# A two-layer gated mixture-of-experts kernel: the second layer's shared expert as one expert of 704, with its weights as the loaded operand

## The reference

```python
# layer 1, xf is 2048 x 512
y = _moe(xf, gate_w, w1, w2, w3)     # 32 experts of 352 inner columns, top 6 of them per row
shared = jax.nn.silu(xf @ sw1) * (xf @ sw3) @ sw2     # sw1, sw3: 512 x 704, sw2: 704 x 512
return (y + shared).reshape(shape)
```

## Time and profile before

| | |
|---|---|
| Median of 3 runs | 1539.49 us (1535.4 to 1543.76) |
| The profiled execution, own time | 1538.83 us |
| Its span in the trace | 1537.0 us |
| TensorE / weight loads / VectorE / ScalarE / GpSimd busy | 85 / 57 / 71 / 51 / 40 % of the span |
| Mean granted TensorE clock | 0.95 of full speed |
| Matmuls | 9124 |

### The profile page before, as it was taken

How to read it: one execution, slowest core, us unless ns; L and a number is a source line. 1 busy time by engine, 2 the same in 40 slices (tenths; PEclk the granted TensorE clock), 3 DMA queues, 4 the chain that set the end, 5 groups by cost and what they waited for, 6 DMA issues and landing times.

```text
span 1537.0 us, 26168 instructions
## 1 busy us (share of the span) xinstructions
PE 1307.7 (85%) x9124; PEld 880.5 (57%) x9124; DVE 1085.1 (71%) x2186; ACT 780.0 (51%) x1451; POOL 616.2 (40%) x478
## 2 busy tenths in 40 slices
PE   0045665589999599999899999999999999999997
PEld 0023352244444365566577777777777777777775
DVE  8999988988989568888655565556656665666432
ACT  3466664645555544442155555555555555555433
POOL 2243443453442244330134444444444445444432
PEclk9988766999999799999999999999999999999999
DMA  3556645679996676551449999998999999999754
GB/s 105 173 164 198 152 117 129 138 181 183 227 241 171 179 212 194 157 167 44 143 125 193 221 202 206 216 208 210 194 216 209 224 188 218 194 231 191 137 101 53
DMA packets 224191, 269.28 MB, mean 175 GB/s; under 512 B 148608, under 2 KB 148736, under 8 KB 223936
## 3 DMA queue, kind: packets, MB, share of 16 engines
q1 hardware_dynamic: 187408, 175.58, 46.2%
q0 software_dynamic: 36656, 92.03, 29.6%
HBM read 167.87 MB, written 70.32 MB: 155 GB/s over the span
## 4 chain that ended last, share of the span: by engine, by line
PE 70%; DVE 22%; issue 5%; ACT 2%; DMA 1%; POOL 0%; POOLq 0%; SPq 0%; ACTq 0%; DVEq 0%
PE psO L2089 22%; PE psG L2018 22%; PE psG L1985 11%; PE psH L2018 5%; DVE FX L1487 5%; PE psG L2024 3%; DVE FX L1469 2%; PE psX L1946 2%; DVE FX L1462 2%; DVE FX L1458 2%; DVE FX L1494 1%; DVE FX L1479 1%; DVE FX L1472 1%; DVE H L1804 1%; PE psX L1884 1%
## 5 line engine op out<-in xcount | busy, mean ns | idle before, releaser
L1166 POOL DMA_INDIRECT out<-OB,posb x128 | 218.9, 1710 | 374.9 <-ACT OB L1395 223.7
L1985 PE MATMUL psG<-Whi,XSp 128*128 128x352 f16 (+2 forms) x952 | 259.6, 363 | 10.0 <-issue 8.2
L2089 PE MATMUL psO<-Whi,RT 128*128 128x512 f16 x768 | 249.7, 380 | 2.3 <-DVE RT L1795 1.9
L2018 PE MATMUL psG<-XSp,Whi 128*128 128x256 f16 x1024 | 170.9, 273 | 1.1 <-ACT XSp L1330 1.1
L2018 PE MATMUL psG<-KW,Whi 128*128 128x256 f16 x1024 | 170.9, 273 | 0.0
L1777 DVE SCALAR_TENSOR_TENSOR RT<-RT,psG 128x256 f32<-128x256 f32 (+1 forms) x154 | 64.7, 420 | 136.1 <-ACT RT L1365 129.1
L1985 PEld LDWEIGHTS psG<-Whi,XSp 128*128 128x128 f16 x952 | 97.9, 103 | 103.7 <-issue 35.7
L1985 PE MATMUL psG<-Wlo,XSp 128*128 128x352 f16 (+2 forms) x476 | 152.0, 364 | 0.0
L2089 PE MATMUL psO<-Wlo,RT 128*128 128x512 f16 x384 | 145.5, 379 | 0.0
L1395 ACT ACTIVATE OB<-psO,WSL 128x512 f32<-128x512 f32 x128 | 87.4, 683 | 111.7 <-PE psO L2089 108.8
L1749 DVE SCALAR_TENSOR_TENSOR Wlo<-FX,Whi 128x1024 f16<-128x1024 f32 x66 | 80.9, 1226 | 89.0 <-ACT Whi L1319 81.7
(11 more groups left out here) (263 smaller groups left out, 2877.4 us busy)
## 6 DMA issues: line engine op xcount, KB each, us to landing
FX<-W SPq DMA_DIRECT2D x66, 544.0 KB
ST<-W SPq DMA_DIRECT2D x64, 544.0 KB
ST<-W SPq DMA_DIRECT2D x23, 512.0 KB
slots<-OB SPq DMA_DIRECT2D x39, 256.0 KB
KW<-fT SPq DMA_DIRECT2D x32, 256.0 KB
xrows<-XG SPq DMA_DIRECT2D x20, 256.0 KB, 3.1
y0rows<-x SPq DMA_DIRECT2D x8, 512.0 KB, 5.3
y0rows<-OB POOLq DMA_DIRECT2D x16, 256.0 KB
```

The source lines that it names most:

```text
L1166: G.indirect_dma_start(out=Y1[:, :], out_offset=bass.IndirectOffsetOnAxis(ap=idx[1][:, j:j + 1], axis=0), in_=OB[o % 4][:, :], in_offset=N ...
L1985: op = M.matmul(o, hx[:, x, q * P:q * P + P], w(half_, off + c, nn), start=first, stop=last)
L2018: op = M.matmul(sums(half_ * 256), W[:, to:to + P], x(which, q), start=(q == 0 and which == 0 and W is Whi), stop=(q == 3 and W is Wlo))
L2089: op = M.matmul(psO[bank(o)][:, :], h(x, q), w(half_, off0 + q * 512), start=(q == 0 and x == 0 and half_ is Whi and first), stop=(q == NK ...
```

## The change

The two halves become one expert of 704, and it is computed the way the routed stage works, with a tile's 128 rows as the streamed operand:

- `parts(b)` replaces `gu_pe`, `h_turn`, `gu`. A tile has three thirds t = 3i, 3i+1, 3i+2. In the slot of an even block stand `f_split` of the previous tile's last third and `f_gu` of third 3i, in the slot of an odd block `f_gu` 3i+1, `f_split` 3i, `f_gu` 3i+2, `f_split` 3i+1.
- `f_gu` on TensorE: third 0 and 1 hold 256 gate and 256 up columns (4 pieces x 4 x 3 = 48 matmuls of 128 streamed columns), third 2 holds 192 gate and 192 up (36 matmuls). They go through the five banks of `f_psum`.
- `f_gu` on ScalarE: a tanh of 256 columns per third; on VectorE two products per third, three in third 2.
- `f_split`: ScalarE casts 256 columns from `H32`, VectorE subtracts 256; for third 2 two subtractions of 128 columns, the first of 64 partitions: the last 64 inner rows' low part lies on the other 64 partitions, and `sw2`'s last 64 rows are stored twice, so one loaded operand holds both.
- `shared_down(b)` stands in the slots of even blocks: all of the previous tile's `down`, 17 matmuls of 512 columns. The semaphore `b_down` rises by 2 there.
- The routed stage's thirds are renumbered by `THIRDS` = 48. The weights are packed in another order by the host. Bytes moved by DMA are the same.

```diff
+THIRDS = 3 * NT
@@ stages()
-    def shared(b, what):
-        if 0 <= b < 32:
-            yield what, S1 + b
+    def parts(b):
+        t = 3 * (b // 2)
+        if b < 0:
+            return
+        if b % 2 == 0:
+            if b:
+                yield "f_split", t - 1
+            yield "f_gu", t
+        else:
+            yield "f_gu", t + 1
+            yield "f_split", t
+            yield "f_gu", t + 2
+            yield "f_split", t + 1
+
+    def shared_down(b):
+        if b % 2 == 0 and b >= 2:
+            yield "down", S1 + b - 1
@@ in a slot
-            yield from shared(b, "gu_pe")
-            if b >= 0:
-                yield from shared(b - 1, "h_turn")
-            yield from shared(b, "gu")
+            yield from parts(b)
...
-                yield from shared(b - 2, "down")
+                yield from shared_down(b)
@@ after table1 and the first three gathers
-    yield from shared(31, "gu")
-    yield from shared(29, "down")
-    yield from shared(31, "h_turn")
-    yield from shared(30, "down")
-    yield from shared(31, "down")
+    yield "f_split", THIRDS - 3
+    yield "f_gu", THIRDS - 1
+    yield "f_split", THIRDS - 2
+    yield "f_split", THIRDS - 1
+    yield "down", R1 - 1
@@ ScalarE, f_gu and f_split
+                if p < 0:
+                    if t >= 2:
+                        eng.wait_ge(b_flo, t - 1)
+                    else:
+                        eng.wait_ge(b_ht, S1)
+                    A.activation(H32[t % 2][:, 0:256], f_psum(t)[:, 0:256], ACT.Tanh,
+                                 scale=0.5 * UN).then_inc(b_ftanh, 1)
+                    return
...
                 eng.wait_ge(b_fh, t + 1)
+                if p < 0:
+                    eng.wait_ge(b_down, S1 + 2 * (t // 3))
+                    A.copy(HSall[:, c * 256:c * 256 + 256], H32[t % 2][:, 0:256]).then_inc(b_fhi, 1)
+                    return
@@ VectorE, f_gu
+                if p < 0:
+                    H = H32[t % 2][:, 0:256]
+                    V.scalar_tensor_tensor(out=H, in0=H, scalar=1.0, in1=ps[:, 0:256], op0=ALU.add,
+                                           op1=ALU.mult).then_inc(b_fsil, 1)
+                    eng.wait_ge(b_fsil, t + 1)
+                    if c == 2:
+                        V.scalar_tensor_tensor(out=H[0:64, 128:256], in0=H[0:64, 128:256], scalar=gain,
+                                               in1=ps[64:128, 128:256], op0=ALU.mult, op1=ALU.mult)
+                    w = 128 if c == 2 else 256
+                    V.scalar_tensor_tensor(out=H[:, 0:w], in0=H[:, 0:w], scalar=gain, in1=ps[:, 256:256 + w],
+                                           op0=ALU.mult, op1=ALU.mult).then_inc(b_fh, 1)
+                    return
@@ VectorE, f_split
+                if p < 0:
+                    H, at, w = H32[t % 2], c * 256, 128 if c == 2 else 256
+                    if c == 2:
+                        V.tensor_tensor(HSall[64:128, 640:768], H[0:64, 128:256], HSall[0:64, 640:768], ALU.subtract)
+                    V.tensor_tensor(HSall[:, 768 + at:768 + at + w], H[:, 0:w], HSall[:, at:at + w],
+                                    ALU.subtract).then_inc(b_flo, 1)
+                    return
@@ TensorE, f_gu
+                if t >= 5:
+                    eng.wait_ge(b_fh, t - 4)
+                if p < 0:
+                    z, ps, wide = S1 + t // 3, f_psum(t), 384 if c == 2 else 512
...
+                    for k in range(wide // P):
+                        for q in range(4):
+                            to = 18432 + 2048 * c + q * wide + k * P
+                            for which, W in ((0, Whi), (1, Whi), (0, Wlo)):
+                                op = M.matmul(ps[:, k * P:k * P + P], W[:, to:to + P],
+                                              XSp[ring(z)][:, which, q * P:q * P + P],
+                                              start=(q == 0 and which == 0 and W is Whi), stop=(q == 3 and W is Wlo))
+                    op.then_inc(b_fgu, 1)
+                    return
@@ TensorE, down
+                elif what == "shared":
+                    eng.wait_ge(b_flo, 3 * (j // 2) + 3)
...
+                if what == "shared" and l == 1:
+                    for k in range(6):
+                        to = 18432 + 5632 + k * 512
+                        for x, half_ in ((0, Whi), (0, Wlo)) + (((1, Whi),) if k < 5 else ()):
+                            op = M.matmul(psO[bank(o)][:, :], HSall[:, x * 768 + k * P:x * 768 + k * P + P],
+                                          half_[:, to:to + 512], start=(k == 0 and x == 0 and half_ is Whi),
+                                          stop=(k == 5 and half_ is Wlo))
+                    op.then_inc(b_down, 2)
+                    return
```

More of the change, by code:

```diff
@@ L535, in stages @@
     yield "r_wts", 7
[L536 to L539, removed]
+    yield from parts(29)
     yield "hot", 18
     yield "hot", 19
-    yield from shared(30, "gu_pe")
-    yield from shared(29, "h_turn")
+    yield from parts(30)
     yield "hot_pe", 18
     yield "hot", 20
-    yield from shared(30, "gu")
     yield "hot_pe", 19
-    yield from shared(28, "down")
+    yield from shared_down(30)
     yield "hot", 21
@@ L551, in stages @@
     yield "hot", 22
-    yield from shared(31, "gu_pe")
-    yield from shared(30, "h_turn")
+    yield "f_gu", THIRDS - 2
     yield "hot_pe", 21
@@ L581, in tile_in @@
         if 0 <= t < 3 * PAIRS:
-            yield what, t
+            yield what, THIRDS + t
     yield "gather", R1 + 3
@@ L1771, in f_gu @@
             def f_gu(t):
-                p, c = divmod(t, 3)
+                p, c = divmod(t - THIRDS, 3)
                 rows = 96 if c == 2 else P
-                H, ps, gain = FH[p % 2][:, c, :], f_psum(t), 0.5 * XS * UN * UN
+                ps, gain = f_psum(t), 0.5 * XS * UN * UN
                 eng.wait_ge(b_ftanh, t + 1)
+                if p < 0:
[10 more added lines that the diff above has]
+                    return
+                H = FH[p % 2][:, c, :]
                 V.scalar_tensor_tensor(out=H[0:rows, :], in0=H[0:rows, :], scalar=1.0, in1=ps[0:rows, 0:256],
@@ L2057, in down @@
                 o, first, last = finished(n)
-                if n < R1:
+                if l == 0:
                     eng.wait_ge(b_hslo, n + 1)
+                elif what == "shared":
+                    eng.wait_ge(b_flo, 3 * (j // 2) + 3)
+                    if j == 1:
+                        eng.wait_ge(*low(34))
+                    first = True
                 else:
-                    eng.wait_ge(b_flo, 3 * (j // 2) + 3)
+                    eng.wait_ge(b_flo, THIRDS + 3 * (j // 2) + 3)
                 if first:
@@ L2137 @@
               np.concatenate([f["L0_ffn_w_down"], f["L0_ffn_sw_down"][None]]), 2)
-    def halves(a):
-        return a.reshape(512, 2, 352).transpose(1, 0, 2)
-    W1 = pack(np.concatenate([f["L1_ffn_w1"], halves(f["L1_ffn_sw1"])]),
-              np.concatenate([f["L1_ffn_w3"], halves(f["L1_ffn_sw3"])]),
-              np.concatenate([f["L1_ffn_w2"], f["L1_ffn_sw2"].reshape(2, 352, 512)]), 3)
+    W1 = np.concatenate([pack(f["L1_ffn_w1"], f["L1_ffn_w3"], f["L1_ffn_w2"], 3), np.zeros((2, 128, 4352), np.float32)])
+    both = np.concatenate([f["L1_ffn_sw1"], f["L1_ffn_sw3"]], axis=1).reshape(4, 128, 1408).transpose(1, 0, 2)
+    cuts = [np.concatenate([np.arange(a, a + 256), np.arange(704 + a, 960 + a)]) for a in (0, 256)]
+    cuts.append(np.concatenate([np.arange(512, 704), np.arange(1344, 1408), np.arange(1216, 1344)]))
+    last = f["L1_ffn_sw2"].reshape(704, 512)
+    downs = [last[k * 128:k * 128 + 128] for k in range(5)] + [np.concatenate([last[640:], last[640:]])]
+    W1[32:34] = np.concatenate([both[:, :, c].reshape(128, -1) for c in cuts] + downs, axis=1).reshape(
+        128, 2, 4352).transpose(1, 0, 2)
     order = np.concatenate([np.arange(352), np.arange(672, 704), np.arange(352, 608)])
```

33 lines of the change are left out of this document (18 added, 15 removed).

## The result

The changed kernel takes 1618.4 us (median of 4) against 1541.6 for the kernel before on the same chip: ratio 1.050, interval [1.049, 1.052]. It is 77 us slower; 12.5 were forecast (1552 against the 1539.5 shown then). The profiled execution has a span of 1616.5 us.

What follows compares the result with a forecast made beforehand. TensorE was taken to set the pace in quiet steps, VectorE in routing ones; +0.5 for two quiet steps, +11.7 for the other steps and +1.6 for the tail gave +13.8 on 1538.83, stated as 1552 us, range 1531 to 1566.

Steps and rivals of the forecast that it cites:

- TensorE's own work: Gate, up, turns and `down` on TensorE at 0.056 us per small matmul: -0.65 us per tile, -10.4 for 16 tiles.
- quiet step: Step of the shared stage where TensorE never idles: 12.95 us before, forecast 13.2, +0.5 for the two together.
- The rival with 0.081: Small matmuls on TensorE take 0.081 us each: +2.7 us per tile, +43, 1582 us; chance 0.08.
- VectorE's own work: Products and subtractions on VectorE grow from 3.17 to 4.10 us, +0.93 per tile.
- the bound of the sum: Upper end for a step with `hot`s: VectorE's 11.94 busy, up to 3.1 added and 0.8 of gaps, +2.4 us.
- between -8 and +19: Ends, in us, for the shared stage's stretch outside the two quiet steps, 186.9 us long before; +11.7 was taken.
- (a): VectorE waits for `psO` in the slot of its `down`: some 2.2 us idle per tile, free where TensorE sets the pace.
- (b): TensorE's `down` waits for the last third's subtraction, behind ScalarE's two weight instructions: 0.9 us.
- routing step: Step with routing and two `hot`s, about 15.5 us before: ends +0.93 and +2.4, middle +1.65 us.
- Tail: End of the shared stage, from last table matmuls to the routed stage: 6.86 us before, 8.5 forecast, +1.6.
- Rival 1: TensorE's gain in the shared stage stays, as VectorE's wait for `psO` falls where it idled: -8 to -11, 1530 us; chance 0.15.
- rival 2: TensorE's gain and the handoff waits cancel in the shared stage: within 5 us of before, 1541 us; chance 0.19.

Runs made afterwards that it cites:

- experiment 3: Changed kernel with VectorE's read of `psO` a slot later and the last third's cast and subtraction a slot earlier: 1582.6 us, ratio 1.027.
- 11: Kernel of experiment 7 with VectorE's low-part subtraction of each third cut to 16 columns: 1560.8 us, ratio 1.012.
- 18: Kernel of experiment 15 with VectorE's low-part subtraction of each third cut to 16 columns: 1549.7 us, ratio 1.006.
- 1: Changed kernel with VectorE's read of `psO` and SyncE's store moved one slot later: 1596.6 us, ratio 1.036.
- 2: Changed kernel with the last third's cast and subtraction moved a slot earlier, ahead of ScalarE's weight instructions: 1592.9 us, ratio 1.034.
- 6: Changed kernel with `down` waiting for each third's subtraction just before the matmuls that use it, no instruction moved: 1576.8 us, ratio 1.023.
- 10: Kernel before with `down` of a tile's two halves gathered in the even block's slot, same work on every engine: 1565.8 us, ratio 1.015.
- experiment 5: Kernel of experiment 3 with three buffers instead of two for the thirds' products (`H32`): 1575.0 us, ratio 1.022.
- 7: Kernel of experiment 5 with the waits by thirds of experiment 6 and the routing's positions moved behind `down`: 1564.4 us, ratio 1.016.
- 15: The best version: kernel of experiment 7 with the logits that follow an odd block put between its two thirds: 1550.3 us, ratio 1.006.
- 16: Kernel of experiment 15 with, in addition, the last five `down` matmuls moved to the head of the odd block's slot: 1560.7 us, ratio 1.012.

## Why the prediction was wrong

- **The place was right, the size was not.** The waits stand where they were forecast, between TensorE and VectorE around `down`; they are several times longer than priced.
- **TensorE's own work: right.** 0.056 us per matmul, and 12.35 for a quiet step of experiment 3 (forecast 12.30). The rival with 0.081 is out.
- **VectorE's own work: right in size, idle in effect.** Its busy time in the stage rose by 19.9 us (14.9 forecast); the instructions that GpSimd held up blur the difference, as both kernels have some. Experiments 11 and 18 price 9 us of it at 3.6 and 0.5 us.
- **The step that failed is the bound of the sum**: "if VectorE paces, 11.94 + 3.1 + 0.8 of gaps = 15.8, +2.4", and from it "anywhere between -8 and +19" for the stretch. I took the worst case to be a full VectorE, and entered the waits (a) and (b) as two separate prices. They are two halves of one ring: (a) delays `x_sum`, that delays ScalarE's `f_tanh`, behind which stand the tanhs of the next thirds, and so (b). A ring's turn is the sum of its links' latencies, whatever each engine's load is, and so it can exceed every sum of busy times. Steps of 16.9 and 22.1 us, with VectorE busy 9.5 and 15.0 and TensorE 14.2 and 14.9, show it; experiments 1, 2, 6 and 10 change only order or waits and no work, and move the time by 22, 25, 42 and 24 us. That order and waits are the cause is so shown. The ring's links were never added up to the whole 77 us: its forecasts for 1, 3, 5, 6 and 7 missed.
- **Wait (a)** was named, at 2.2 us per tile; it was 66/16 = 4.1, of which some 1.5 is that `down` ran partly at the lower clock (5.1 us and not 3.66 in the tile shown). The remark that it is free "where TensorE sets the pace" is false: the quiet step s = 4 lost 4.0 us where +0.25 was forecast. (The routing step s = 6 lost 6.5 where +1.65 was.)
- **Wait (b)** was priced at 0.9 us and only in quiet steps; it was 3.2 on average over 13 tiles. Missed in it: the 1.7 us that a subtraction loses beside GpSimd, four times in the stage, a loss that the kernel before already shows at 646.33; the two buffers of `H32` (experiment 5); the place of the thirds' tanh behind `f_tanh`.
- **The clock** was not in the sum. It is lower behind the pauses (0.86 against 0.97 over the stage) and 1.00 in experiment 3's quiet steps, which have none; by the estimate above it costs about 29 of the 77 us. No run separates it from the pauses.
- **Tail:** forecast 8.5 us; from the last table matmuls (831.93) to 842.33 it was 10.4, for 6.86 before. The 17 `down` matmuls took 5.4 of it, not 3.66: from 837.42 to 840.81 the granted clock was 0.50.
- **The addition:** +13.8 on 1538.83, and 0.7 more for the median, is 1553.3; 1552 was said. It changes nothing.
- Rival 1, TensorE's gain stays, and rival 2, the two cancel, are false; experiment 3's quiet steps show where the gain would have been.

What stays open: the last 9 us of the best version, whose stage still has 29 us of idle TensorE (18 before) and a granted clock of 0.92 (0.97 before); why 16 is slower than 15 by 10 us; and the part ahead of the stage, whose end lay between 520.7 and 527.9 us in the profiled runs though no edit touches it (4.2 of the 79.5 us between the two profiled executions).

## What to carry to other kernels

When work is gathered into fewer, longer pieces, follow one item once round all engines' queues, from release to the same release, and add the latencies, including what stands ahead in each in-order queue; compare that with the step, before any sum of busy times. Waiting for the part that the next instruction needs, not for the whole, moved no instruction and gave 42 of the 77 us here. A microsecond taken off an engine is worth what stands close behind it: the same cut of GpSimd's work gave 14.8 us in one order and 2.4 in the other. A reordering can be tested in the old kernel alone, with no work changed.

## What the runs showed of the hardware

A VectorE subtraction with both operands in SBUF and 64x128 elements took 2.0 to 2.2 us in four of its 16 instances in the changed kernel, each while GpSimd's 128x1024 subtraction (2.1 us) ran, and 0.28 to 0.35 in the other twelve. VectorE's `ex<-ex,mask` (128x128) did the same in the kernel before: 2.23 us beside GpSimd, 0.29 to 0.32 with GpSimd's work cut. Cutting that work gave 14.8, 11.8 and 2.4 us in three kernels.

Matmuls with 128 streamed columns and a fresh weight load each kept 0.056 us over 84 in a row at full clock. After a pause of TensorE of 4.5 us (560.2 to 564.7) the granted clock was 0.54 until 568.00, with matmuls of 512 columns 0.43 us apart, and then 1.00, with 0.2155. After the last tile's pause of 2.6 us the first two of them still started 0.22 and 0.24 us after one another; then the clock was 0.50 until 840.81.
